# When VectorE makes the low parts of the second-layer expert weights

## What is computed

```
tok = x.reshape(-1, d)                                    # 4096 tokens, d = 256
gate = jax.nn.softmax(tok @ Wgate.T, axis=-1)             # 8 experts
vals, idx = jax.lax.top_k(gate.T, k_cap)                  # each expert takes its 512 best tokens
g = _ln(tok[idx_flat], mlp_g, mlp_b).reshape(k_cap, E, d)
y = jnp.einsum('ked,ehd->keh', g, fc1s) + b1s             # first layer, 256 -> 1024
y = jax.nn.gelu(y, approximate=True)
y = jnp.einsum('keh,edh->ked', y, fc2s) + b2s             # second layer, 1024 -> 256
y = y * w[..., None]
tok = tok.at[idx_flat].add(y.reshape(-1, d))
```

## Time and profile before

| | before |
|---|---|
| median of 3 runs | 1495.05 us (1495.02 to 1495.63) |
| profiled execution | 1500.34 us, its span 1498.5 us |
| mean granted TensorE clock | 0.972 |
| TensorE busy | 1400.3 us, 93% |
| VectorE busy | 969.0 us, 65% |
| ScalarE busy | 1032.7 us, 69% |
| GpSimd busy | 921.5 us, 61% |

### The profile page before, as it was taken

One profiled execution on the slowest core, in us unless ns is written; L12 is line 12 of the kernel. 1 busy time (PEld: TensorE's weight loads), 2 busy tenths in 40 slices (PEclk: granted clock), 3 DMA queues, 4 the chain that ended last, 5 costly groups with the idle time before them and its releaser, 6 DMA issues. The chain is left out here.

```text
span 1498.5 us, 30098 instructions
## 1 busy us (share of the span) xinstructions
PE 1400.3 (93%) x10714; PEld 1181.2 (79%) x10714; DVE 969.0 (65%) x2243; ACT 1032.7 (69%) x2729; POOL 921.5 (61%) x864
## 2 busy tenths in 40 slices
PE   4799999997899999999999999999998987999896
PEld 3799999985677777777787778777875777888885
DVE  5876767634666667667666766766664677677652
ACT  4556665556889888888988888898887500756542
POOL 3577666645767866876777687677767402454342
PEclk9899999998999999999999999999999999999997
DMA  5342222110100110111011011101100173254421
GB/s 154 94 139 64 71 66 71 47 46 12 36 9 29 51 43 9 50 51 34 18 51 43 21 38 50 43 8 50 38 21 29 40 286 103 46 149 99 114 36 21
DMA packets 61781, 89.16 MB, mean 59 GB/s; under 512 B 6160, under 2 KB 51136, under 8 KB 58944
## 3 DMA queue, kind: packets, MB, share of 16 engines
q1 hardware_dynamic: 53376, 75.96, 15.6%
q0 software_dynamic: 6144, 8.39, 3.5%
q10 hardware_dynamic: 2112, 2.88, 0.6%
HBM read 62.03 MB, written 25.18 MB: 58 GB/s over the span
## 5 line engine op out<-in xcount | busy, mean ns | idle before, releaser
L1302 POOL TENSOR_TENSOR prob<-prob,share_p 128x512 f32<-128x512 f32 x256 | 272.2, 1071 | 215.1 <-DVE share_p L1410 215.1
L1404 DVE TENSOR_REDUCE shift<-bank 128x2 f32<-128x512 f32 x256 | 164.7, 685 | 244.2 <-PE bank L1050 244.2
L1189 ACT ACTIVATE prob<-bank,shift 128x256 f32<-128x256 f32 x512 | 236.8, 485 | 81.4 <-DVE shift L1404 81.4
L147 PE MATMUL bank<-wqkv_h,rowsT_h 128*128 128x512 f32 x384 | 161.1, 419 | 6.7 <-PEq L306 3.5
L147 PE MATMUL bank<-wqkv_h,rowsT_l 128*128 128x512 f32 x384 | 152.5, 397 | 0.0
L147 PE MATMUL bank<-wqkv_l,rowsT_h 128*128 128x512 f32 x384 | 152.5, 397 | 0.0
L1076 PE MATMUL bank<-pT,landing 128*64 128x256 f32 x1024 | 141.0, 397 | 11.0 <-ACT pT L1262 11.0
L1063 PE MATMUL bank<-ident,prob 128*128 128x128 f32 x1024 | 141.3, 281 | 0.1
L1290 POOL TENSOR_TENSOR landing<-landing,rq 128x512 f32<-128x512 f32 x128 | 130.8, 1043 | 9.5 <-DVE rq L1358 9.4
L1063 PEld LDWEIGHTS bank<-ident,prob 128*128 128x128 f32 x1024 | 110.3, 142 | 18.2 <-issue 0.8
L1076 PEld LDWEIGHTS bank<-pT,landing 128*64 128x64 f32 x1024 | 62.7, 137 | 66.8 <-issue 22.7
(11 more groups left out here) (295 smaller groups left out, 4624.2 us busy)
## 6 DMA issues: line engine op xcount, KB each, us to landing
landing<-in_fc1s SPq DMA_DIRECT2D x6, 1024.0 KB
landing<-in_fc2s SPq DMA_DIRECT2D x6, 1024.0 KB
rows<-in_x SPq DMA_DIRECT2D x16, 256.0 KB, 2.9
xT<-in_xT SPq DMA_DIRECT2D x16, 256.0 KB, 2.6
x_again<-in_x SPq DMA_DIRECT2D x16, 256.0 KB, 2.7
x_rows<-x SPq DMA_DIRECT2D x16, 256.0 KB, 3.1
rows<-x_rows SPq DMA_DIRECT2D x16, 256.0 KB, 3.1
x<-x_rows SPq DMA_DIRECT2D x16, 256.0 KB, 2.9
```

The costliest lines, as they stand in the source:

```text
L147: last = nc.tensor.matmul(out, a, b, start=(n == 0), stop=(n == 3 * len(ks) - 1))
L1189: last = nc.scalar.activation(prob[at][:, n, :], score_bank[side][:, n * T:(n + 1) * T], ACT.Exp, bias=shift[:, at, n:n + 1], scale=-1.0, ...
L1302: nc.gpsimd.tensor_tensor(prob[at][:, :, :], prob[at][:, :, :], share[:, at, :].unsqueeze(2).to_broadcast([P, TT, T]), ALU.mult).then_inc( ...
L1404: nc.vector.tensor_reduce(shift[:, s % 2 * 2 + side, :], score_bank[side][:, :].rearrange("p (n m) -> p n m", n=TT), AX, ALU.min).then_inc ...
```

## The change

The low part of an expert's second-layer weights is still made by VectorE, in four pieces of 128 x 512. Before, expert `t`'s pieces are made in step `t` itself (steps 2 to 7), one behind each odd `hid_l`. Now expert `t + 1`'s pieces are made in step `t` (steps 1 to 6), all four in a row between `weigh(t, 1)` and `weigh(t, 2)`. The number of instructions is the same, 24, and so are their waits' kinds: each waits for its high part, now counted in the same step.

```
@@ in VectorE's step, in the loop over the groups m
                         if there(t) and there(new) and not first(t) and m % 2 == 0:
                             q = m // 2
                             dve.wait_ge(w_hi, t * 8 + q - 7)
...
-                        if there(t) and there(t - 2) and m % 2 == 1:
-                            q = m // 2
-                            dve.wait_ge(w_hi, t * 8 + q - 11)
-                            vec.tensor_tensor(piece(w2_l[odd], q), w2_raw[odd][:, q * 512:(q + 1) * 512],
-                                              piece(w2_h[odd], q).bitcast(F32), ALU.subtract).then_inc(w2_in[odd], 8)
@@ behind weigh(t, 0) and weigh(t, 1)
+                    if there(t) and there(new) and not first(t):
+                        for q in range(4):
+                            dve.wait_ge(w_hi, t * 8 + q - 3)
+                            vec.tensor_tensor(piece(w2_l[1 - odd], q), w2_raw[1 - odd][:, q * 512:(q + 1) * 512],
+                                              piece(w2_h[1 - odd], q).bitcast(F32), ALU.subtract).then_inc(w2_in[1 - odd], 8)
                     if there(t):
                         weigh(t, 2, odd)
                         weigh(t, 3, odd)
```

## The result

The changed kernel takes 1475.61 us in the median (1471.2 to 1476.81) against 1495.22 (1495.02 to 1495.63) of the kernel before: ratio 0.9863, 95% interval 0.9843 to 0.9884, or 20.5 us (17.3 to 23.5) less. Forecast were 1472.8 us, 22.2 less, and 1470.5 to 1482.

The account below looks back on a forecast made before the run. TensorE was taken to bound the kernel, stalled by VectorE's `ew_l`. 13.3 us of idle time plus 8.9 of low clock, with zero added cost, made 22.2 us off the median 1495.05: 1472.8 us, range 1470.5 to 1482.

Parts of the forecast that it names:

- What bounds: TensorE, busy 1400 us, sat idle 13.3 us in six waits for VectorE's last `ew_l` piece, queued behind the eighth `hid_l` subtraction.
- Step 1 as the model: Expert step 1 lacks the wait and takes 24.5 us between first-layer ends; later steps were priced as their excess over it.
- the sum: Gain over the later expert steps: 22.2 us, taken off the median 1495.05 to give 1472.8 us; chance 0.80.
- Its two halves: The 22.2 us over the expert steps were split into 13.3 us of TensorE idle time and 8.9 us of low clock.
- the rival's 1482: In the expert steps the low clock remains without idle time; only 13.3 us are gained, 1481.8 us; chance 0.09.
- The added part: Four moved subtractions, 2.7 us, before the third weighed sum fit into VectorE's 2.87 us of idle time; cost zero.
- The fourth rival: Late VectorE sums hold back the next phase: 2.7 us a step at most, 13.5 us back, 1486.3 us; chance 0.03.
- The clock does come back: Denies the rival that TensorE's low clock stays in the expert steps, 1481.8 us; chance 0.09.
- The wait does not change hands: Denies the rival that TensorE then waits for the eighth `hid_l` subtraction, gaining only 4.1 us, 1490.9 us; chance 0.03.
- GpSimd is touched a little: One or two `idle` operations lengthen GpSimd's chain by up to 1.6 us; the rival through late scatters: 1501 us, chance 0.03.
- the 2.8 us of room: Spare between the model step's last scatter landing, near 1331.7, and VectorE's next `share` copy asking for it at 1334.5.

Follow-up runs that it names:

- the kernel that works in its waits: The kernel before with 8 (steps 2 to 5) or 11 (steps 6 and 7) identity products on TensorE ahead of the second layer's wait: 1492.16 us, ratio 0.9947.

## Why the prediction was right, and which term had no firm ground

**What bounds.** Right. The wait of the earlier trace rows was the whole waiting part, and the fourth piece the whole of the wait: moving it alone gives the ratio 0.9855, leaving it alone 1.0002.

**Step 1 as the model.** Right to 0.1 us: stretches of 24.5 us before and 24.49 after, and the last 96 matmuls at the pace assumed. From step 1 on the two profiles differ by 22.6 us, where the sum had 22.2; that is so close partly because the sum read the clock's loss off this very profile. The spans differ by 24.5, since the changed kernel's profile was already 1.9 us earlier at step 1 (1305.79 against 1307.74) by what lies ahead.

**Its two halves.** The waiting was put at 13.3 and is 14.0 by the kernel that works in its waits. The clock was put at 8.9 and is 8.6 in that profile, and 6.0 and 4.5 in two others with the same stalls.

**The term without firm ground.** The sum was made against a profile of 1500.34 us and then taken unchanged off a median of 1495.05, with the remark that none of the edits touches the difference. That was not safe, since the clock's part differs between executions: 8.6, 6.0 and 4.5 us in three profiles with the same stalls, and the sum's 8.9 came from the one with the largest. The timed gain, 20.5 us, less the 14.0 of waiting leaves 6.5 us for the clock, or 3.3 to 9.5 by the interval of the gain; the kernel that works in its waits gives 8.0 (4.5 to 11) for the same part. Both hold 8.9, so it is not shown that the term was too large for the timed runs. How much of the 5.3 us between that profile and the median was the clock is open too: its step 1 began at 1307.74, late among the 1302.8 to 1308.5 of all profiles here. Of the 2.8 us by which the forecast of 1472.8 was low, 0.9 is the difference between the ratio (20.5 us) and the medians (19.6), 0.2 the later median of the kernel before (1495.22), and the remaining 1.7 lies within the interval of the gain. That the forecast came so near is therefore in part luck: with the third profile's 4.5 us of clock the same working gives a gain of 18.5. The range allowed for one slow stretch more at its lower end; for fewer of them, as in the two later profiles, it had no term, and only the rival's 1482 covered them.

**The added part.** Right, and with far more room than was claimed. Cover of 2.87 us for 2.7; measured 2.54 with 0.30 left. Beyond it, the sums can be 5 us late at no cost. The fourth rival had 2.7 us of lateness cost 2.7; the kernel with four more subtractions shows zero for 2.2 us.

**The rivals.** The clock does come back: 1.00 throughout. The wait does not change hands, as step 1 said. GpSimd is touched a little, and by another instruction than the prediction had. It let one or two of the `idle` operations fall beside the moved subtractions. In steps 1 to 4 none does (one does in steps 5 and 6, of 0.41 and 0.93 us). Instead the third gather starts with them and takes 1.45 or 1.46 us, against 0.95 in the model step; the fourth, which starts in their last 0.7 us, is not lengthened. In the changed kernel's step 2, whose moved subtractions run from 1340.82 to 1343.36:

```profile
1340.89 1.46 POOL L1831 DMA_INDIRECT gx<-x_rows,next_index  x1 [0.30 <-issue]
1342.65 0.96 POOL L1831 DMA_INDIRECT gx<-x_rows,next_index  x1 [0.30 <-issue]
1343.61 0.21 POOL L1818 TENSOR_TENSOR idle<-idle 128x1 f32<-128x1 f32 x1
...
1350.71 2.04 POOL L1839 DMA_INDIRECT out<-eyw,index  x1 [0.16 <-POOL idle L1818]
```

and in the model step of the kernel before:

```profile
1318.35 0.95 POOL L1831 DMA_INDIRECT gx<-x_rows,next_index  x1 [0.30 <-issue]
```

The last scatter's issue ends 22.5 us behind the index product of its step (1330.28), 0.8 later than in the model step (1329.41 against 1307.74), inside the 2.8 us of room. The Trainium skill's page "SBUF — State Buffer", section "Who interferes with whom", has GpSimd instructions that read SBUF contend with a VectorE instruction of two SBUF inputs, but it also infers that generating a DMA's descriptors isn't touched by such a subtraction. The third gather (1.46 against 0.95 us) does not fit that inference; which part of it was held up, and by what, was not tried apart.

## What to carry to other kernels

Where an engine waits for the last of several pieces, look at what stands ahead of that piece in its maker's queue, and move that one; the maker's load mattered here only beyond 8 extra subtractions a step, and a reorder within the phase can do as well as a move out of it. If one pass of the loop happens to lack the suspected wait, price every other pass against it. And a short stall of TensorE cost a third to two thirds of its length again in clock here (4.5 to 8.6 us for 14.0), in a way that differs between executions: take that part from several profiles, not from one that is slower than the median.

## What the runs showed of the hardware

The same stalls of 1.95 and 2.8 us brought five, four and three slow stretches of six in three profiles, each up to 1.6 us (2.7 for the last); small matmuls in the stall kept the clock at 1.00 in all six. Twelve waits listed at no more than 0.6 us brought none. A float32 product of the 128-column identity is two matmul records and took 0.236 us at a clock of 1.00 (32 records in 3.77 us). And the third gather on GpSimd took 1.46 us where it started with VectorE's moved subtractions, 0.95 where VectorE was idle.
